# A two-layer graph network on one core: layer one cut into five zones of target widths instead of two

## What is computed

```python
h = relu(layernorm(x))
msgs = edge_weight[:, None] * (h @ W + b)[src]            # layer one
agg = segment_sum(msgs, dst) / (segment_sum(edge_weight, dst) + 1e-6)
x = x + relu(agg)
h = relu(layernorm(x))
m = gelu(concat(h[src], edge_attr) @ W_msg + b_msg)       # layer two
x = x + gelu(((1 + eps) * h + segment_sum(m, dst)) @ W_upd + b_upd)
```

## Time and profile before

| | us |
|---|---|
| median of 3 runs | 2678.9 |
| lowest and highest | 2669.0, 2679.41 |
| span of the profiled execution | 4082.0 |
| of it up to the first sums of layer one (copy of `xs`, line 735) | 112.3 |
| bodies 1 to 15 of layer one (15 intervals between these copies) | 458.0 |
| bodies 16 to 48 (33 intervals) | 1236.9 |
| from there to the steady part of layer two | 72.8 |
| layer two, steady part | 2160.0 |
| tail | 42.0 |

### The profile page before, as it was taken

How to read it: one execution, slowest core, us unless ns; L and a number is a source line. 1 busy time by engine, 2 the same in 40 slices (tenths; PEclk the granted TensorE clock), 3 DMA queues, 4 the chain that set the end, 5 groups by cost and what they waited for, 6 DMA issues and landing times.

```text
span 4082.0 us, 72599 instructions
## 1 busy us (share of the span) xinstructions
PE 2950.6 (72%) x22325; PEld 2600.4 (64%) x22326; DVE 2089.7 (51%) x4376; ACT 1607.4 (39%) x5144; POOL 1835.1 (45%) x1911
## 2 busy tenths in 40 slices
PE   2776766665665666576788788778878878878887
PEld 2666665554554555565677677677767767767777
DVE  8444445544544554544455455555545545555554
ACT  2343333433433443334344444444434444444443
POOL 2333344334434434424455545545545554554552
PEclk9888787877777777787888888888888888888888
DMA  4000000000000000002333333333333333333332
GB/s 92 14 12 14 13 16 16 13 13 15 14 12 15 15 13 14 15 14 66 75 84 85 81 81 84 87 79 83 88 76 86 83 81 81 84 87 78 85 88 52
DMA packets 473123, 214.39 MB, mean 53 GB/s; under 512 B 264996, under 2 KB 442024, under 8 KB 473076
## 3 DMA queue, kind: packets, MB, share of 16 engines
q1 hardware_dynamic: 412404, 151.55, 14.2%
q0 software_dynamic: 60672, 62.25, 9.2%
HBM read 208.14 MB, written 5.51 MB: 52 GB/s over the span
## 4 chain that ended last, share of the span: by engine, by line
PE 41%; issue 11%; another core or an unknown queue 1%; DVE 1%; DVEq 0%; ACT 0%; ACTq 0%
PE ps L918 28%; PE ps L1123 6%; PE ps L988 5%; PE ps L1112 2%; DVE sel L1451 0%; PE ps L1070 0%; DVE rows L1455 0%; DVEq L1464 0%; PE ps L1017 0%; ACT eT L844 0%; DVE sums_sb L1472 0%; DVE parts L1219 0%; DVE room L1654 0%; ACT dw L652 0%
## 5 line engine op out<-in xcount | busy, mean ns | idle before, releaser
L629 POOL DMA_INDIRECT rows<-p_table,idx x1176 | 1109.4, 943 | 1065.6 <-ACT idx L660 736.0
L918 PE MATMUL ps<-parts,pick_all 128*128 128x448 f32 x5488 | 1241.0, 379 | 63.5 <-issue 59.9
L629 POOL DMA_INDIRECT rows<-h_table,idx x720 | 709.5, 985 | 1062.1 <-ACT room L760 857.7
L918 PEld LDWEIGHTS ps<-parts,pick_all 128*128 128x128 f32 x5488 | 1046.3, 195 | 193.6 <-issue 109.4
L947 PE MATMUL ps<-adj,h_sb 128*64 128x160 f32 (+1 forms) x4802 | 503.4, 342 | 516.4 <-issue 469.9
L947 PEld LDWEIGHTS ps<-adj,h_sb 128*64 128x64 f32 x4802 | 404.4, 170 | 608.8 <-issue 551.9
L1451 DVE TENSOR_TENSOR sel<-ps,mask 128x896 f32<-128x896 f32 x196 | 213.5, 1089 | 761.4 <-remote 541.9
L1388 DVE TENSOR_SCALAR hot_p<-iota_p,scal 128x256 fp32r<-128x256 f32 (+1 forms) x848 | 309.4, 365 | 410.9 <-PE ps L928 321.6
L928 PE MATMUL ps<-hot_c,hot_p 128*128 128x125 f32 (+1 forms) x2336 | 456.3, 302 | 87.6 <-issue 72.4
L721 ACT COPY adj<-ps 128x500 f32<-128x500 f32 (+1 forms) x848 | 389.8, 524 | 203.0 <-PE ps L928 126.5
L928 PEld LDWEIGHTS ps<-hot_c,hot_p 128*128 128x128 f32 x2336 | 377.4, 207 | 110.5 <-issue 86.5
(11 more groups left out here) (181 smaller groups left out, 2975.9 us busy)
## 6 DMA issues: line engine op xcount, KB each, us to landing
src_all<-keys SPq DMA_DIRECT2D x196, 448.0 KB
ea<-in_edge_attr_dram SPq DMA_DIRECT2D x196, 256.0 KB
rows<-p_table,idx POOLq DMA_INDIRECT x1176
rows<-h_table,idx POOLq DMA_INDIRECT x720
x_sb<-in_x_dram SPq DMA_DIRECT2D x6, 224.0 KB, 3.5
h_table<-h_sb SPq DMA_DIRECT2D x6, 224.0 KB
p_table<-h_sb SPq DMA_DIRECT2D x6, 224.0 KB
out_dram<-h_sb SPq DMA_DIRECT2D x6, 224.0 KB
```

Of the source, the lines that this page charges most:

```text
L629: nc.gpsimd.indirect_dma_start(out=rows[:, s, j, 0:D], out_offset=None, in_=table[:, :], in_offset=bass.IndirectOffsetOnAxis(ap=idx[:, s, ...
L918: last = nc.tensor.matmul(to, hot[:, k, t * P:(t + 1) * P], parts[:, part, k, :, :].rearrange("p a d -> p (a d)"), start=(k == 0 and part ...
```

## The change

Layer one has five zones. (bodies, `JA`, `WT`, `WP`) are (8, 5, 3, 1), (8, 5, 4, 1), (8, 5, 6, 2), (8, 4, 8, 2) and (17, 4, 10, 2). So bodies 16 to 23 go from 4 to 5 adjacency tiles a group, and have 3 gathers a group instead of 4; bodies 24 to 31 keep 4; bodies 32 to 48 stay as they are. `lo_rows` gets memory of its own. Only the first zone's part of it is loaded and waited for ahead of line 1330; the other zones' 18 small DMAs come on SP after the first loads of `src_bc`, and DVE waits for them, and makes their rows of `dst_tab`, behind the `mask` of layer two. ACT waits for that once, ahead of its first body.

```diff
-    for bodies, ja, wt, wp in ((16, 5, 5, 1), (BODIES - 16, 4, 10, 2)):
+    for bodies, ja, wt, wp in ((8, 5, 3, 1), (8, 5, 4, 1), (8, 5, 6, 2), (8, 4, 8, 2), (BODIES - 32, 4, 10, 2)):
...
-        lo_rows = early[:, KH * P + 3 * PICKS * P:KH * P + 3 * PICKS * P + NG]
+        lo_rows = sb("lo_rows", [P, NG])
...
-            for z in ZONES:
+            def load_rows(z, done):
                 for j in range(z.JA):
                     sp.dma_start(lo_rows[j * z.WT:(j + 1) * z.WT, z.groups],
                                  least[j:j + 1, z.groups].to_broadcast(
-                                     [z.WT, (z.end - z.first) * SLOTS])).then_inc(s_leastr, 16)
+                                     [z.WT, (z.end - z.first) * SLOTS])).then_inc(done, 16)
+            load_rows(ZONES[0], s_leastr)
...
             for q in range(2):
                 load_bc(0, q)
+            for z in ZONES[1:]:
+                load_rows(z, s_rowsr)
...
+            act.wait_ge(s_rows, len(ZONES) - 1)
             for start, end, zones in STRETCHES:
...
-            dve.wait_ge(s_leastr, 16 * (1 + sum(z.JA for z in ZONES)))
+            dve.wait_ge(s_leastr, 16 * (1 + ZONES[0].JA))
...
-            for z in ZONES:
-                n = z.group_cols
-                meta(nc.vector.scalar_tensor_tensor(out=dst_tab[0:n, J, z.groups], ...
+            meta(row_targets(ZONES[0]))
...
+            dve.wait_ge(s_rowsr, 16 * sum(z.JA for z in ZONES[1:]))
+            for z in ZONES[1:]:
+                row_targets(z).then_inc(s_rows, 1)
             dve.wait_ge(s_zero, 1)
```

More of the change, by code:

```diff
@@ L414, in two_layer_gnn @@
         s_leastr = sem("tile_least_targets_read")
+        s_rowsr = sem("later_zones_least_targets_read")
+        s_rows = sem("later_zones_rows_ready")
         s_scan = sem("tile_numbers_made")
@@ L1338, in _, with row_targets @@
             meta(nc.vector.memset(dst_tab[:, J, :], -20000))
-            for z in ZONES:
+            def row_targets(z):
                 n = z.group_cols
-                meta(nc.vector.scalar_tensor_tensor(out=dst_tab[0:n, J, z.groups], in0=lo_rows[0:n, z.groups],
-                                                    scalar=place[0:n, z.index:z.index + 1],
-                                                    in1=base_bc[0:n, z.groups], op0=ALU.add, op1=ALU.subtract))
+                return nc.vector.scalar_tensor_tensor(out=dst_tab[0:n, J, z.groups], in0=lo_rows[0:n, z.groups],
+                                                      scalar=place[0:n, z.index:z.index + 1],
+                                                      in1=base_bc[0:n, z.groups], op0=ALU.add, op1=ALU.subtract)
+            meta(row_targets(ZONES[0]))
             meta(nc.vector.tensor_copy(high_i[:, :, :], src_tab[:, 0:JA, :]))
```

## The result

The changed kernel's median is 2655.7 us (7 runs, 2647.6 to 2670.3), the kernel before's 2678.9 beside it (7 runs, 2669.0 to 2683.9). The ratio on record is 0.9948, with an interval of 0.9928 to 0.9969: some 14 us faster (8 to 19), about the 0.5% that the prediction set as its bound. "No change" was wrong, though 2655.7 lies in the range of 2640 to 2704.

The account below looks back on a forecast made before the run. DVE was taken to lead in both zones, POOL level in the second, PE behind. Terms +1.8 - 3.5 - 2.4 + 4.0 - 1.6 + 2 = +0.3 gave 2679 us, own range 2666 to 2692, with rivals 2640 to 2704.

Parts of the forecast that it names:

- No change: Whole kernel: forecast 2679 us against a median of 2678.9, with a chance of 0.48 for the same time.
- off the path, since DVE leads: Bodies 1 to 7: line 947 saves PE 1.3 us a body, counted as nothing because DVE leads.
- -5.9 forecast for bodies 1 to 15: Narrower `hot_c` on DVE: -3.5 us in bodies 1 to 7 and -2.4 us in bodies 8 to 15.
- +4.0 forecast: Bodies 16 to 23: DVE's 20 tiles take the place of the saved gathers, +0.5 us in each of eight.
- rebuilt PE body of 15.8: First zone: PE's work in a body put at 15.8 us, behind DVE's 17.1 and POOL's 16.1.
- rival (a): Layer one: PE or its clock was the bound, so line 947's saving pays, 2635 us; chance 0.2.
- -1.6: Bodies 24 to 31, `WT` 8: DVE saves a little, gathers stay, 8 x -0.2 us (0 to -6.4).
- rival (c): Bodies 16 to 31: PE goes cold after waiting about 4 us for `rows_of_sums`, +3 us a body, 2725 us; chance 0.15.
- The check in the prediction: Whole kernel before: rebuilt stretches, with layer two at 7.5 us a group or 1470 us, make 2660, 0.7% under the median.
- The start: Ahead of the first sums: more tables on DVE, fewer loads waited for, together +1.8 us (0 to +5).
- (b): Second zone: the gathers led alone, so bodies 16 to 23 fall to DVE's 22 us, 2667 us; chance 0.15.
- the forecast case: Whole kernel: the prediction's own sum of 2679 us, range 2666 to 2692; chance 0.5.

Follow-up runs that it names:

- experiment 14: The changed kernel plus, in bodies 16 to 23, twelve idle PE products ahead of the fifth tile and eighteen ahead of the first windows: 2657.3 us, ratio 0.9933.
- experiment 1: The kernel before, unchanged, run again for a second profile: 2669.6 us, span 2667.8.
- experiment 5: The kernel before plus two unused buffers (64 bytes a partition ahead of the mask, 784 ahead of the tile bounds): 2660.0 us, ratio 0.9966.
- experiment 9: The kernel before, unchanged, run a third time for its profile: 2670.6 us.
- experiment 10: The kernel before plus one unused buffer of 64 bytes a partition ahead of the mask table: 2659.1 us, ratio 0.9942.
- experiment 11: The kernel before plus one unused buffer of 64 bytes ahead of the node features `x_sb`, behind the mask: 2656.0 us (one run).
- experiment 4: The changed kernel, but bodies 16 to 23 keep 4 tiles a group with `WT` 8: 2648.6 us, ratio 0.9898.
- experiment 7: The changed kernel with the old two zones, so late loads into a buffer of their own without the new zones: 2663.4 us, ratio 0.9967.
- experiment 8: The changed kernel, but bodies 16 to 23 write their weights in one part instead of two: 2628.8 us, ratio 0.9847.

## Why the prediction was wrong, point by point

**Which steps failed.** One term was put at nothing without being worked out: layer two was taken as untouched, though the diff moves its buffers, and its picks became 10.4 us shorter. That is the largest part of the gain. In layer one two terms had the wrong bound: line 947 was left out as "off the path, since DVE leads" (-5.9 forecast for bodies 1 to 15, -13.5 measured), and the clock in bodies 16 to 23 was left to a rival (+4.0 forecast, +11.6 measured). These two errors nearly cancel, so it is luck that layer one's own sum came within 1.3 us of the forecast. Bodies 32 to 48 (-4.7) and the stretch between the layers (-3.1) stay open.

**The first zones' sums were not off the path.** The prediction saw that line 947 saves 1.3 us a body (measured: 1.37) and left it out, "since DVE leads". It does not lead there. The rebuilt PE body of 15.8 was too short by 1.0: it priced line 928 at 3.50/32 = 0.109 us from a window in which nothing else ran, and in a body 40 of them take 4.91, 0.12 each, and the sums 4.50 for 4.3. DVE in turn was rebuilt at 17.1, and has 14.72 of work plus its waits, 2.2 us in four bodies of them for PE. With 15.8 and 17.1 the order of the two was wrong. That 17.1 was the body's measured length is luck: it came out because 1.3 us were added to DVE for twelve gathers here, where the second zone got 0.7 for sixteen. Line 928, said to save nothing, saved a little too (4.91 to 4.63 for 40). That is rival (a), in the first zone only: it asked 1.3 a body, and the six inner bodies gave 1.3 each. With the border body it makes -7.3 for -3.5. Bodies 8 to 15: -6.2 for -2.4, with the same line at `WT` 4; I take it to be the same reason.

**The second zone was read rightly.** In bodies 24 to 31, before and after:

```profile
613.41 6.98 PE L947 MATMUL ps<-adj,h_sb 128*64 128x160 f32 x98
```

```profile
614.32 5.67 PE L955 MATMUL ps<-adj,h_sb 128*64 128x128 f32 x98 [0.28 <-ACT adj L728]
```

`WT` 8 for 10 takes 1.3 us a body from PE, as `WT` 3 for 5 did in the first zone, but here the body moves by 0.4 only, and there by 1.3. So here PE is not the bound. -3.4 is in the range given for -1.6. The undisturbed windows say the same: in the first zone PE is busy for 98% of a body and DVE for 86%, in the second 88% and 89%. In the disturbed windows of the earlier trace rows PE was the busier one in both zones.

**Bodies 16 to 23: rival (c), at a sixth of its price, on top of the forecast.** DVE's tile is what the sum said, 0.26 + 0.27 + 0.27 from start to start, the answer to the tile of the earlier trace rows:

```profile
470.79 0.34 DVE L1399 TENSOR_SCALAR hot_p<-iota_p,scal 128x256 fp32r<-128x256 f32 x1
471.05 0.35 DVE L1401 TENSOR_SCALAR hot_c<-iota_c,scal 128x150 fp32r<-128x150 f32 x1
471.32 0.35 DVE L1401 TENSOR_SCALAR hot_lo<-iota_c,scal 128x150 fp32r<-128x150 f32 x1
471.59 0.34 DVE L1399 TENSOR_SCALAR hot_p<-iota_p,scal 128x256 fp32r<-128x256 f32 x1
```

and its busy time of 19.4 to 20.0 is near the 20 foretold. At nearly full clock, and with the idle products in it, a body is 21.7 us long (experiment 14), +0.5 against before: as near as these runs come, that is the forecast's +4.0 for eight. The two bodies of the change that run at 1.00 throughout take 21.0 each, so the idle products, or what the bodies between them hand on, may be in the 21.7. What the forecast left to a rival is the clock. PE waits, and then this:

```profile
431.13 1.19 PE L996 MATMUL ps<-onehot,room 128*65 128x72 f32 x16 [1.75 <-DVE room L1440]
```

```profile
411.70:432.20 20.50, 17.90 (x227) 17.13 (x226) 18.10 (x72) 12.28 (x49) 14.03 (x13) 1.00 0.10 19
432.20:442.40 10.20, 10.20 (x55) 10.12 (x54) 9.97 (x39) 5.55 (x21) 5.10 (x6) 0.50 0.09 16
442.40:448.10 5.70, 5.68 (x104) 5.37 (x102) 4.30 (x19) 2.31 (x12) 3.63 (x4) 1.00 0.10 17
```

A wait of 1.75 us for `rows_of_sums`, the one that rival (c) named with about 4, then 10.2 us at 0.50 with PE busy throughout. Its products of line 936 start 0.21 us apart there, and 0.11 ahead of the wait. PE falls behind, its next wait is gone, the clock comes back, and with it the wait. So the bodies swing between 21.0 and 24.7, and the first, whose wait is 3.4 us, takes 25.8. The clock's price is 181.2 - 173.9 = 7.3 us or a little more for the eight. (If the whole excess over 21.0 is the clock's, it is 13 us.) The prediction priced it at +3 us in 16 bodies, 48 us. The mistake in it: in bodies 24 to 31, with 16 tiles, the clock stays at 0.84 to 1.00 and a body at 20.2 to 21.5 us, so half of its sixteen bodies cost nothing, and in the others the swing gives back every second time what it took. The prediction let a single cold stretch of 3 us hide in PE's slack; here single ones last 3.4 to 20.5 us.

What makes the clock fall is only in part shown. The waits do not do it alone, for the kernel before has this one too, in every body from 18 on (experiment 1), 1.2 to 1.8 us long and at a granted clock of 1.00:

```profile
413.03 1.44 PE L988 MATMUL ps<-onehot,room 128*65 128x72 f32 x20 [1.67 <-DVE room L1429]
```

PE idles no less there, 1.4 to 2.6 us a body in bodies 17 to 23 against 0.2 to 2.4 in the change. Idle products in the waits do bring the clock back (experiment 14), so what PE does around a wait counts; which property of the new bodies tips it stays open. By the Trainium skill's "TensorE: Matmul & The Clock Gate", section "HAM oscillation — how this bites in real kernels", each burst behind a long wait would start cold. In bodies 16 to 23 of the change the trace agrees: the six with a wait of over 1 us (1.1 to 3.4) all have a stretch at half clock (3.4 to 20.5 us), and the two without, 17 and 20, stay at 1.00. In the kernel before it does not: behind waits of the same length PE stays at 1.00.

**Memory moved, and the prediction did not price that.** The diff takes `lo_rows` out of `adj`'s memory, and I read that as a wait that becomes shorter. It also moves every later buffer. In layer two, where PE has no gap at all, this is worth 10.4 us, more than half of the result. Experiments 5, 9, 10 and 11 show it without the rest of the change: nothing but buffer places differs, and the picks go from 1513.8 and 1514.0 to 1503.6, 1503.5 and 1503.3. The check in the prediction had layer two bound by POOL's gathers at 7.5 us a group, 1470 us in all; it is bound by PE at 7.7, 1514. That the check still came within 0.7% is luck: the start, the stretch between the layers and the tail came from the disturbed execution and were some 35 us too long (windows of the steady part, of before and after):

```profile
1150.00:2600.00 1450.00, 1450.00 (x10517) 1330.28 (x10516) 1083.73 (x1127) 870.58 (x2531) 1076.28 (x1141) 1.00 0.48 119
```

```profile
1150.00:2600.00 1450.00, 1450.00 (x10571) 1339.27 (x10570) 1092.19 (x1133) 876.74 (x2552) 1083.43 (x1149) 1.00 0.49 120
```

**Bodies 32 to 48, -4.7 us: open.** They take 356 to 359 us in all kernels that have one of the new zones, and 360 to 363 in the kernel before, with or without moved buffers, and with late loads alone. One row differs in DVE's timeline of such a body, before and after:

```profile
909.93 0.06 DVE L1492 MEMSET tick<- 1x1 f32 x1 [0.21 <-issue]
```

```profile
905.55 0.06 DVE L1503 MEMSET tick<- 1x1 f32 x1
```

A gap of 0.21 us with nothing waited for stands there 16 times in these 17 bodies before, 3.4 us in all, and once after (0.4 us). But the kernel of experiment 4 has 14 such gaps (2.7 us) and takes 357.0 all the same, so I don't call it the cause. The -3.1 between the layers is within what this stretch varies by among kernels with the same code there (56.3 to 63.9).

**The start** took +4.3, in its range of 0 to +5. The wait for the first zone's loads (before and after) answers to that of line 1330 in the earlier trace rows:

```profile
56.54 1.18 DVE L1330 TENSOR_TENSOR rel_tab<-dst_tab,src_raw 128x980 int16<-128x980 int16 x1 [4.80 <-DMA adj<-least]
```

```profile
57.51 1.18 DVE L1338 TENSOR_TENSOR rel_tab<-dst_tab,src_raw 128x980 int16<-128x980 int16 x1 [1.96 <-DMA lo_rows<-least]
```

It ends 0.2 to 1.0 us later than in the two profiles of before, for 1.4 forecast. What the late loads bring can't be told: the start is 103.5 with them alone (experiment 7) and 103.6 with nothing but moved buffers (experiment 5), against 104.7 and 105.3 before. Against experiment 7 the three further zones cost 5.8 us, where the sum had 2.8 + 1.2 + 1.3 less what it gave back; which part was mis-sized no run shows.

**The chances.** (a), half of (b) and a tenth of the forecast case add up to 0.33, and not to 0.34.

## What to carry to other kernels

When an engine is to be called "off the path", compare what a body gives back, or where the other engine waits for it, and not two rebuilt sums that lie within 10% of each other. A change that gives one engine more to do between two points at which TensorE waits is to be priced with the clock as well: here one write less of VectorE per tile (experiment 8) turned 22.7 us a body into 19.1, though TensorE's own work grew. And in a stretch that TensorE fills alone, a buffer added elsewhere can be a change of its own: time the old kernel with that much padding before the gain is put down to the idea.

## What was not expected of the hardware

The time of a pick product depends on where buffers lie that it doesn't touch: 28 of them take 5.92 or 6.02 us. `parts` and `pick_all` have the same addresses in all the padded kernels; what moved are buffers that ACT, DVE and the gathers write beside them. 64, 800 and 864 bytes mend all groups, 128 bytes half of those that were slow, and the remainder of 64 does not decide. What holds the product there no run shows; that the writes of the others do it is a guess. The Trainium skill's "SBUF — State Buffer", section "SBUF: two separate sides", says that PE never waits for another user of the memory. If the guess is right these rows speak against that, and the measurement decides; if not, another mechanism ties PE's pace to places that it doesn't touch.

A wait of PE as short as 1.75 us was followed by 10.2 us at half clock in one body of the change, and one of 1.24 us by 6.8. In the kernel before, waits of 1.2 to 1.8 us stand in every body from 18 on, and the clock stays at 1.00.
